# First attention stage: score groups two ahead, and a new order of the work on TensorE, VectorE and ScalarE

## The reference, cut to what matters

```python
qkv = x @ w_qkv.T                                  # 16 heads of 32
scores = q @ k.T * 32 ** -0.5 + alibi              # causal: masked scores are -10000
num = 0.5 * (1 + scores * rsqrt(1 + scores * scores))
probs = num / (sum(num) + 1e-6)                    # rational softmax
out = (probs @ v) @ w_out.T
```

## Time and profile before

| | us |
|---|---|
| median of 3 runs | 3233.4 |
| the profiled execution | 3229.13 |
| its span | 3227.3 |
| first stage, from the first values product to the first OUT product behind iteration 7 | 52.34 to 732.59 |
| cross attention and experts | the rest |

### The profile page before, as it was taken

How to read it: one execution, slowest core, us unless ns; L and a number is a source line. 1 busy time by engine, 2 the same in 40 slices (tenths; PEclk the granted TensorE clock), 3 DMA queues, 4 the chain that set the end, 5 groups by cost and what they waited for, 6 DMA issues and landing times. The chain is left out here.

```text
span 3227.3 us, 50841 instructions
## 1 busy us (share of the span) xinstructions
PE 3018.3 (94%) x19312; PEld 2477.8 (77%) x19312; DVE 1646.6 (51%) x3608; ACT 1348.0 (42%) x2298; POOL 700.2 (22%) x721
## 2 busy tenths in 40 slices
PE   5889998978999999999999949999999999999997
PEld 4667777756788777778777738888888888888886
DVE  5888888873556556666566633333333333333321
ACT  5677777764555555555555511111111111111111
POOL 0000000011111221112121033243434343434332
PEclk9889999989999999999999969999999999999999
DMA  3011111123111111111111022141313131313122
GB/s 100 24 35 44 37 45 45 46 82 121 42 50 38 45 38 56 51 38 42 41 52 34 25 74 75 54 97 55 96 55 96 56 95 56 95 57 94 57 71 37
DMA packets 93875, 189.72 MB, mean 59 GB/s; under 512 B 17568, under 2 KB 27552, under 8 KB 91712
## 3 DMA queue, kind: packets, MB, share of 16 engines
q1 hardware_dynamic: 79168, 158.68, 16.1%
q0 software_dynamic: 14592, 29.43, 5.1%
HBM read 140.25 MB, written 47.82 MB: 58 GB/s over the span
## 5 line engine op out<-in xcount | busy, mean ns | idle before, releaser
L1777 ACT ACTIVATE f_hf<-f_h 128x448 f32<-128x448 f32 x256 | 139.4, 544 | 1014.1 <-PE f_h L1804 958.0
L1748 DVE CAST f_hh<-f_hf 128x448 fp32r<-128x448 f32 x256 | 105.9, 414 | 847.0 <-ACT f_hf L1777 822.0
L1819 PE MATMUL f_y<-f_w2h,f_hh 128*128 128x512 f32 x896 | 357.5, 399 | 0.0
L1819 PE MATMUL f_y<-f_w2h,f_hl 128*128 128x512 f32 x896 | 354.0, 395 | 0.0
L1819 PE MATMUL f_y<-f_w2l,f_hh 128*128 128x512 f32 x896 | 352.2, 393 | 0.0
L1707 POOL TENSOR_TENSOR f_w1l<-f_raw,f_w1h 128x512 fp32r<-128x512 f32 x128 | 182.4, 1425 | 778.6 <-DVE f_w1h L1731 778.5
L1396 ACT ACTIVATE c_s_sb<-c_s_sb,c_nmx 112x750 f32<-112x750 f32 x256 | 236.1, 922 | 159.6 <-DVE c_nmx L1239 156.6
L1388 ACT COPY c_pT<-psum 125x672 f32<-125x672 f32 x256 | 184.6, 721 | 224.3 <-PE psum L1496 223.2
L1804 PE MATMUL f_h<-f_xTh,f_w1h 128*128 128x448 f32 x1024 | 255.2, 371 | 2.9 <-DVE f_xTl L1736 1.4
L1496 PEld LDWEIGHTS psum<-a_ident,c_s_sb 112*125 112x125 f32 x1536 | 193.5, 189 | 79.9 <-issue 76.2
L1804 PE MATMUL f_h<-f_xTl,f_w1h 128*128 128x448 f32 x1024 | 250.7, 366 | 0.0
(11 more groups left out here) (252 smaller groups left out, 5766.6 us busy)
## 6 DMA issues: line engine op xcount, KB each, us to landing
f_raw<-in_w SPq DMA_DIRECT2D x128, 512.0 KB, 4.2
h_craw<-in_ctxT SPq DMA_DIRECT2D x16, 1125.0 KB, 5.1
a_x_in<-in_x SPq DMA_DIRECT2D x9, 896.0 KB, 5.5
a_xr<-in_x SPq DMA_DIRECT2D x8, 896.0 KB, 6.0
x_dram<-a_xr SPq DMA_DIRECT2D x8, 896.0 KB, 4.8
q_dram<-a_q SPq DMA_DIRECT2D x32, 224.0 KB, 5.4
h_q<-q_dram SPq DMA_DIRECT2D x16, 448.0 KB, 5.4
c_x<-x_dram SPq DMA_DIRECT2D x16, 448.0 KB, 4.9
```

What stands on the lines that cost most here:

```text
L1748: dve.tensor_copy(hs[0][:, l % 2, c * HC:c * HC + HC], hf[:, c, :]).then_inc(h_hi, 1)
L1777: act.activation(hf[:, c, :], H[:, 0:HC], ACT.Gelu_apprx_tanh).then_inc(free, 1)
L1819: mm = pe.matmul(Y[t][:], hs[a][:, l % 2, 128 * t:128 * t + 128], w2s[b][:, l % NSLOT, :], start=j == 0 and q == 0, stop=last_of_expert(l) ...
```

## The change

`PLAN` is laid out anew, with K3 and Q3 earlier (Q3 goes to the slot 7 before, K3 to slot 0) and OUT1 in slot 4 beside OUT0. On TensorE a slot is now: values s, first half, scores of group s+2, second half. On VectorE it is: output s and its low part, transposes, `refine`, product of group s+2, first residual, `root_error` (the old L490), second residual, numerator of group s+2, then the statistics. On ScalarE: reciprocal s, off_diagonal s+1, first half's evacuations, high part of output s, `root_of`, roots of group s+2, second half's evacuations, normalise. `normalise(1, ...)` is cut in two halves, one in slot 1 and one in slot 2. The SP queue's code is unchanged. Number and size of the instructions of an iteration stay the same.

```diff
@@ -218,25 +218,25 @@
-    PLAN = {0: (["Q3", "T2c3"], ["OUT2", "OUT3"]),
-            1: (["K3"], ["V2", "V3", "T1c0"]),
+    PLAN = {0: (["K3", "T2c3"], ["OUT2", "OUT3"]),
+            1: (["V2"], ["V3", "T1c0"]),
             2: (["Z0", "T1c1"], ["Z1"]),
             3: (["Z2", "T1c2"], []),
-            4: (["Z3", "T1c3"], ["OUT0"]),
-            5: (["Q0", "T2c0"], ["K0", "OUT1"]),
-            6: (["Q1", "T2c1"], ["K1", "V0"]),
-            7: (["V1", "T2c2"], ["Q2", "K2"])}
-    PLAN_LAST = {0: (["Q3", "T2c3"], ["OUT2", "OUT3"]),
-                 1: (["K3"], ["V2", "V3"]),
+            4: (["Z3", "T1c3"], ["OUT0", "OUT1"]),
+            5: (["Q0", "T2c0"], ["K0", "Q1"]),
+            6: (["K1", "T2c1"], ["V0", "Q2"]),
+            7: (["V1", "T2c2"], ["K2", "Q3"])}
+    PLAN_LAST = {0: (["K3", "T2c3"], ["OUT2", "OUT3"]),
+                 1: (["V2"], ["V3"]),
                  2: (["Z0"], ["Z1"]),
                  3: (["Z2"], ["Z3"]),
-                 4: (["T2e0"], ["OUT0"]),
-                 5: (["T2e1"], ["OUT1"]),
+                 4: (["T2e0"], ["OUT0", "OUT1"]),
+                 5: (["T2e1"], []),
                  6: (["T2e2"], ["CK00", "CK01", "CK10"]),
                  7: (["T2e3"], ["CK11", "CK20"])}
                "second": ("T2c3", "Z0", "Z1", "Z2", "Z3")}
-    START = ["T1c0", "T1c1", "T1c2", "T1c3", "Q0", "K0", "Q1", "K1", "V0", "V1", "Q2", "K2"]
+    START = ["T1c0", "T1c1", "T1c2", "T1c3", "Q0", "K0", "Q1", "K1", "V0", "V1", "Q2", "K2", "Q3"]
     def units(kind, s, half):
@@ -485,9 +485,11 @@
             dve.wait_ge(r_made, i * NG + n + 1)
             dve.tensor_tensor(num[n % 2], sc[0:R, :, 0:NPAIR], r_sb, ALU.mult).then_inc(p_made, 1)
-        def numerator(i, n):
+        def root_error(i, n):
             dve.wait_ge(rr_made, i * NG + n + 1)
             dve.scalar_tensor_tensor(u_sb, u_sb, 1.0, q_sb, ALU.add, ALU.mult).then_inc(m_made, 1)
+
+        def numerator(i, n):
             dve.wait_ge(p_made, i * NG + n + 1)
             dve.wait_ge(m_made, i * NG + n + 1)
             dve.scalar_tensor_tensor(num[n % 2], u_sb, 3.0, num[n % 2], ALU.subtract, ALU.mult).then_inc(y_made, 1)
@@ -510,14 +512,15 @@
                               ALU.subtract).then_inc(o_lo, 1)
         def residual(i, kind, unit, n):
-
             j = int(unit[3])
             dve.wait_ge(xr_loaded, n * 16 + 16)
             dve.wait_ge(gen_full, product_number(i, kind, unit) + 1)
             b = BANK[kind, unit]
             dve.tensor_tensor(xr[:, j, :], xr[:, j, :], gen[b][0:R, :], ALU.subtract).then_inc(gen_free[b], 1)
-            dve.wait_ge(gen_free[b], uses_before(i, kind, unit) + 1)
-            statistics(1, xr, j, stats_made[1])
+
+        def residual_statistics(i, kind, unit):
+            dve.wait_ge(gen_free[BANK[kind, unit]], uses_before(i, kind, unit) + 1)
+            statistics(1, xr, int(unit[3]), stats_made[1])
         def lo_of_weights(k):
             dve.wait_ge(w_hi, k + 1)
@@ -544,33 +547,41 @@
         aggregate(0, stats_first, 2)
         product_signed(0, 0)
         refine(0, 1)
+        root_error(0, 0)
         numerator(0, 0)
+        product_signed(0, 1)
+        root_error(0, 1)
+        numerator(0, 1)
         for n in range(4, len(pieces)):
             split_piece(n)
         def body(i, kind):
             for s in range(NG):
-                late = [u for u in units(kind, s - 1, 1) if u[0] == "T"] if s > 0 else []
-                if s > 0:
-                    lo_of_output(i, s - 1)
-                elif kind != "first":
-                    lo_of_output(i - 1, NG - 1)
-                for unit in late:
-                    lo_of_transpose(i, kind, unit)
-                if has_step(kind, s + 1):
-                    product_signed(*step(i, s + 1))
-                    numerator(*step(i, s + 1))
+                for unit in units(kind, s - 1, 1) if s > 0 else ():
+                    if unit[0] == "T":
+                        lo_of_transpose(i, kind, unit)
+                output(i, s)
+                lo_of_output(i, s)
+                for unit in units(kind, s, 0):
+                    if unit[0] == "T":
+                        lo_of_transpose(i, kind, unit)
                 if s == 0 and kind in ("second", "mid"):
                     refine(0, i + 1)
                 if s == 1 and kind != "first":
                     refine(1, i - 1)
-                output(i, s)
-                for unit in units(kind, s, 0):
-                    if unit[0] == "T":
-                        lo_of_transpose(i, kind, unit)
-                for unit in units(kind, s, 1):
-                    if unit[:3] == "OUT":
-                        residual(i, kind, unit, i - 1 if unit in ("OUT2", "OUT3") else i)
+                outs = [u for u in units(kind, s, 1) if u[:3] == "OUT"]
+                if has_step(kind, s + 2):
+                    product_signed(*step(i, s + 2))
+                for unit in outs[:1]:
+                    residual(i, kind, unit, i - 1 if s == 0 else i)
+                if has_step(kind, s + 2):
+                    root_error(*step(i, s + 2))
+                for unit in outs[1:]:
+                    residual(i, kind, unit, i - 1 if s == 0 else i)
+                if has_step(kind, s + 2):
+                    numerator(*step(i, s + 2))
+                for unit in outs:
+                    residual_statistics(i, kind, unit)
                 if s == 0 and kind != "first":
                     aggregate(1, stats_made[1], i)
                 if s in (6, 7) and kind != "last":
...
@@ -596,12 +607,13 @@
             act.wait_ge(mv_made[half], n * TPI + TPI)
             act.activation(rstd[half][:], mv[half][:, :, 1], ACT.Abs_reciprocal_sqrt, bias=eps[0:R, 0:1]).then_inc(root_made[half], 1)
-        def normalise(half, n, src, dst):
+        def normalise(half, n, src, dst, *js):
             act.wait_ge(rstd_made[half], n + 1)
-            for j in range(TPI):
+            for j in js or range(TPI):
                 ins = act.activation(dst[:, j, :], src[:, j, :], ACT.Identity, bias=shift[half][:, j:j + 1],
                                      scale=rstd[half][:, j:j + 1])
-            ins.then_inc(xn_made[half], 1)
+            if j == TPI - 1:
+                ins.then_inc(xn_made[half], 1)
         def hi_of_transpose(i, kind, unit):
             dst, c = (xT if unit[1] == "1" else x2T), int(unit[3])
@@ -680,39 +692,35 @@
         for unit in ("V0", "V1"):
             evacuate(0, "start", unit)
         off_diagonal(0, 0)
-        evacuate(0, "start", "Q2")
+        roots(0, 1)
+        for unit in ("Q2", "K2"):
+            evacuate(0, "start", unit)
+        evacuate(0, "start", "Q3")
         for n, (src, dst, k) in enumerate(pieces[4:], 4):
             act.wait_ge(w_loaded[4 + n % 4], 16 * (n // 4 + 1))
             act.copy(dst[0][:, k, :], work[:, n % 4, :]).then_inc(w_hi, 1)
-        evacuate(0, "start", "K2")
         normalise(0, 1, x_in, x_in)
         def body(i, kind):
             for s in range(NG):
-                if s > 0:
-                    hi_of_output(i, s - 1)
-                elif kind != "first":
-                    hi_of_output(i - 1, NG - 1)
+                reciprocal(i, s)
                 if has_step(kind, s + 1):
-                    roots(*step(i, s + 1))
+                    off_diagonal(*step(i, s + 1))
+                for unit in units(kind, s, 0):
+                    evacuate(i, kind, unit)
+                hi_of_output(i, s)
                 if s == 0 and kind in ("second", "mid"):
                     root_of(0, i + 1)
                 if s == 1 and kind != "first":
                     root_of(1, i - 1)
-                reciprocal(i, s)
-                for unit in units(kind, s, 0):
+                if has_step(kind, s + 2):
+                    roots(*step(i, s + 2))
+                for unit in units(kind, s, 1):
                     evacuate(i, kind, unit)
-                late = units(kind, s, 1)
-                for unit in late[:1]:
-                    evacuate(i, kind, unit)
-                if s == 1 and kind in ("second", "mid"):
+                if s == 0 and kind in ("second", "mid"):
                     normalise(0, i + 1, x_in, x_in)
-                if s == 2 and kind != "first":
-                    normalise(1, i - 1, xr, xn2)
-                if has_step(kind, s + 1):
-                    off_diagonal(*step(i, s + 1))
-                for unit in late[1:]:
-                    evacuate(i, kind, unit)
+                if s in (1, 2) and kind != "first":
+                    normalise(1, i - 1, xr, xn2, 2 * s - 2, 2 * s - 1)
                 if kind == "last" and s in (2, 4):
                     for n in range(3):
                         handover.hi_of_piece(act, n + 3 * (s // 4))
...
@@ -846,31 +853,35 @@
         run(0, "start", "K1")
         made(0, "start", "Q0", "K0")
         scores(0, 0)
-        for unit in START[8:]:
+        for unit in ("V0", "V1"):
             run(0, "start", unit)
```

(31 more changed lines are left out.)

## The result

| | before | after |
|---|---|---|
| median, us (range) | 3233.32 (3229.09 to 3235.1) | 3293.59 (3290.99 to 3294.36) |
| the profiled execution | 3229.13 | 3293.21 |
| first stage, to the first OUT product behind iteration 7 | 732.59 | 799.76 |

The ratio is 1.0191, with a 95% interval of 1.0178 to 1.0204: the changed kernel is slower, by about 1.9%. The forecast was 3287, within 3250 to 3312.

The account below looks back on a forecast made before the run. A closed 9.92 us loop through ScalarE and VectorE was taken as the bound. Iterations 2 to 6 +45.3, iteration 1 +6.3, iteration 0 +2.5, iteration 7 +2: +56 on 3229.13, plus 2 for the median, gives 3287 us, range 3250 to 3312.

Parts of the forecast that it names:

- The loop is not opened; a slot costs at least 9.92: ScalarE-VectorE ring from `o_made` through high part, roots and numerator to the next output: stays closed, at least 9.92 us a slot.
- Residuals and statistics: VectorE, slots 0 and 4: two units each now stand between L486 and the next output, +2.27 us a slot.
- `aggregate`, statistics of x, T1c0, `root_of`: Work moved into the loop, us (slots): `aggregate` 0.48 (0, 7), x 1.19 (6, 7), T1c0 0.54 (1), `root_of` 0.2 (0, 1).
- T1c1 and the low clock: Slot 2: TensorE's T1c1 waits for T1c0's low part, then group 4's scores run at half clock, delaying roots: +1.26 us.
- Z2 behind the store: Slot 3, iterations 2 to 6: ScalarE's Z2 evacuation waits for Z0's store, holding up high part and roots: +4.0 us.
- Start and iteration 0: Before the first `o_made`: 0, bounds -4 to +4 us; iteration 0, `o_made` 0 to 7: 74.7 against 72.19, +2.5 us.
- Iteration 7: Last iteration, up to the first OUT product: 91.6 us against 89.65, +2 us.
- The signs: Wrong if L486 waits under 2 us in slots 3 and 5; TensorE's waits for `o_made` should grow.
- Rival A: Loop rules, but the T1c1 low-clock and Z0-store ties are not met: 28 us less, 3259; chance 0.17.
- Rival B: TensorE's trailing eats its 1.5 us in three slots of six iterations: +27 us, 3312; chance 0.12.
- Rival C: Two-group lead ends TensorE's waits, its own work bounds: iteration 77.2 us or less, -45 us, 3186; chance 0.07.
- Rival D: The change moves the waits and no time, each addition replacing an equal wait: 3233 us; chance 0.02.

Follow-up runs that it names:

- experiment 5: Changed kernel with Z0's store early, roots s+2 and first-half evacuations earlier on ScalarE, low parts of output and late transposes behind root_error on VectorE; 3186.33 us, ratio 0.9868.
- Experiment 8: Kernel before, lead of one group kept: roots s+1 ahead of high part of output s-1, low part between root_error and numerator; 3244.48 us, ratio 1.0034.
- experiments 3 and 4: Changed kernel plus two VectorE statistics in slot 5: in 3 behind the numerator, 3307.92 us; in 4 ahead of the product, 3294.78 us.
- experiment 1: Changed kernel with the store of Z0 issued on the SP queue ahead of the wait for normalise and the load of xr; 3274.05 us, ratio 1.0133.
- experiment 2: Changed kernel with T1c0's low part on VectorE moved from behind slot 1's numerator to between root_error and numerator; 3283.66 us, ratio 1.0165.
- experiment 7: Experiment 5 with the last iteration's four loads of the next stage's weights ahead of Z0's store and the wait for normalise; 3180.04 us, ratio 0.9848.

## Why the prediction held, step by step

The mechanism held; that the total came so close is partly luck. Up to the first OUT product behind iteration 7 the profiled execution grew by 67.2 us where 56 was forecast, 8.9 of the difference in iteration 7, and the later stages' -3.2 hid part of it.

- **The loop is not opened; a slot costs at least 9.92.** Right, and shown from both sides. Slot 5 is 9.92 or 9.93 in every iteration, no slot of a full iteration is under it, and experiment 5 has slots of 7.6 and 8.2. It takes away the tie on ScalarE (roots behind the high part) and leaves the one on VectorE (output behind the numerator). Experiment 8, with nothing but the roots and the low part moved, took slot 3 of the kernel before from 9.93 to 8.07, so these two moves together open the loop.
- **Residuals and statistics, +2.27.** Measured 12.11 less 9.92 = 2.19. That it is the place and not the work that costs was shown by experiments 3 and 4, on the statistics; the residuals have only the slots of the changed kernel as evidence.
- **`aggregate`, statistics of x, T1c0, `root_of`.** Slots 0, 1, 6 and 7 were forecast at 12.87, 10.66, 11.11 and 11.59 and measured at 12.76, 10.64, 11.12 and 11.92. Only slot 7 was off, by 0.33 in iterations 2 to 5; in iterations 0, 1 and 6 it was 11.58 to 11.60. The same 0.3 stays in experiment 1, so Z2's wait isn't its cause, nor is TensorE: VectorE's first instruction of the output starts 0.61 to 0.65 us behind the start of `aggregate` in these four and 0.29 in the others, in a gap that no wait fills. Those four are the passes at whose end the program's loop (it runs iterations 2 to 6) goes back to its start; that this jump is the cause fits, but was not tried.

```profile
427.76 0.38 DVE L462 BATCH_NORM_AGGREGATE a_mv<-a_stats 112x2 f32<-112x6 f32 x4
428.39 0.39 DVE L503 SCALAR_TENSOR_TENSOR a_dt<-psum,a_rden 128x224 f32<-128x224 f32 x1 [0.25 <-issue]
```

- **T1c1 and the low clock, +1.26.** TensorE idled 5.51 us where "some 5" was said, and the granted clock behind it was 0.50. Slot 2 lost 1.46, and experiment 2 gave 1.45 back. The term was 0.2 too small.
- **Z2 behind the store, +4.0.** Slot 3 measured 3.74 to 4.24 more than 9.92 in iterations 2 to 6 and nothing more in iteration 1, which has no Z. Experiment 1 gave it all back in these iterations. What stands ahead in the queue is what the store's time was made of, as the prediction argued: 6.15 us behind the load of `xr`, so the row was the one to take. The rule of the Trainium skill's page "DMA: Bandwidth & Descriptors", section "Anatomy of one DMA", about 2.0 us plus bytes over 436 GB/s for the software-driven path, gives an estimate of 2.5 us for 224 KB and would have had slot 3 only 0.6 over the loop. The store issued by itself in experiment 1 landed in 2.1 us, not far from it; behind the load it did not.
- **Start and iteration 0.** 0.85 and 2.7, forecast 0 and 2.5.
- **Iteration 7: the one term that was mis-sized.** +10.9 against +2. Slots 0 to 2 came as forecast (12.57, 10.11 and 17.55 against 12.67, 10.12 and 17.8). Slot 3 took 15.32 where 9.92 stood, slot 4 14.49 where 12.19 stood, and from `o_made` 6 to the first OUT product it was 8.95 instead of 7.4. The first of them, in ScalarE's timeline: Z2 waited for its store here too, which the forecast had only for iterations 2 to 6. It puts the high part of output 3, which could have started at the end of its output at 751.08, at 752.74.

```profile
752.30 0.54 ACT L646 ACTIVATE a_q<-psum 128x448 f32<-128x448 f32 x1 [2.69 <-DMA q_dram<-a_q]
752.74 0.37 ACT L672 CAST a_oTh<-a_o_sb 128x224 fp32r<-128x224 f32 x1
```

  That is 1.6 us, and in experiment 1 slot 3 was 13.71, 1.6 less (slot 2 was 0.8 longer there, where the weights came later). What is left of slots 3 and 4, 3.8 and 2.4 us, is VectorE's own instructions taking longer, below. Slot 2 holds 0.8 of the same (L506 takes 1.18 instead of 0.39 from 749.90 on), so that it came out at 17.55 is partly luck; the wait for the weights was 6.6 instead of 7.2. The 1.55 by which the last stretch ran over was not followed.
- **The signs.** L486 waited 1.7 us in slots 3 and 5, under the 2 that the prediction had set as a sign of being wrong. The sign was set wrongly: the low part of a transpose (0.6 us) lies under the cover in these slots and takes up part of the wait, while from the start of the high part to L486 it is still 3.06 us (384.45 to 387.51, in slot 4) against 3.05. TensorE's waits for `o_made` were to grow and fell, from 53.2 to 35.2 us; what grew instead is its wait for the low part of the transposes (T), 49.4 us:

```profile
PE psum L839 <- DVE a_o_sb L506: 35.2, 13, 9.4
PE psum L763 <- DVE a_xTl L481: 49.4, 12, 8.2
```

- **The chances.** Rival A's two ties were both met. Rival B has no row for it: ScalarE's roots waited for scores 7 times in the stage, 6.2 us in all, which is the T1c1 wait of slot 2 and nothing else. (Its 3312 adds 27 to 3285; from the 3287 of the forecast it is 3314.) Rival C at 0.07 described a kernel one step away from this one, and it was right to hold it low for these lists. That experiment 5 ended at its 3186 is partly luck: against the kernel before iterations 2 to 6 gained 29.4 where C had 35.5, iteration 1 gained 3.8 where it had 6, and iteration 0 gained 8.2 where it had 3. Rival D had its reason stated and failed by it.

## What to carry to other kernels

Cut a pipelined loop at one semaphore and ask of each slot which engines it goes round; where two in-order lists close a ring, work inside the ring costs its full time and work in the gap nothing until the gap is full (experiments 3 and 4), whatever the mean busy shares say. In this kernel more lead for a third engine brought nothing while the ring was closed, and opening the ring brought nothing while that engine had a lead of one group (experiment 8); so try both together. A moved evacuation or high part also moves behind every wait on its new way, a DMA store's among them.

## What the runs showed of the hardware

In iteration 7 of the changed kernel VectorE's instructions take up to twice their time. Its timeline, and GpSimd's beside it:

```profile
757.25 1.55 DVE L490 SCALAR_TENSOR_TENSOR a_ew<-a_ew 112x1344 f32<-112x1344 f32 x1
758.90 2.97 DVE L495 SCALAR_TENSOR_TENSOR a_ew<-a_ew 112x1344 f32<-112x1344 f32 x1
761.91 2.58 DVE L497 SCALAR_TENSOR_TENSOR a_ew<-a_ew,a_keep 112x896 f32<-112x896 f32 x1
...
771.55 2.52 DVE L490 SCALAR_TENSOR_TENSOR a_ew<-a_ew 112x1344 f32<-112x1344 f32 x1
774.00 0.67 DVE L519 TENSOR_TENSOR a_xr<-a_xr,psum 112x512 f32<-112x512 f32 x1
```
```profile
758.32 7.84 POOL L108 TENSOR_TENSOR h_cTl<-h_craw,h_cTh 128x750 fp32r<-128x750 f32 x3 [7.50 <-ACT h_cTh L103]
771.39 6.35 POOL L94 TENSOR_TENSOR h_wvl<-h_stage,h_wvh 128x512 fp32r<-128x512 f32 x3 [5.24 <-ACT h_wvh L89]
```

L495 took 1.56 elsewhere and L497 1.09, while the same GpSimd work spans 5.54 and 3.90 us in the kernel before, where it meets only short instructions of VectorE (they grow too, L504 from 0.39 to 1.65). Both engines lose while they overlap, and ahead of 758.32 L490 has its usual 1.55. Only instructions that read both inputs from SBUF are long; L519, which reads one of them from PSUM, has its usual 0.67 in the midst. The excess of L495, L497 and L506 in slot 3 adds up to 3.8 us, that of L490, L495 and L497 in slot 4 to 2.4. By the Trainium skill's page "SBUF — State Buffer", section "Who interferes with whom", a VectorE instruction with two inputs in SBUF contends with a GpSimd instruction that reads SBUF; the trace agrees. In the loop this time counts in full. No experiment here took GpSimd's work away, but experiment 7 moved it: its first group starts at 638.09, spans 5.39 us instead of the 3.73 of experiment 5, and meets `numerator`'s last instruction, which takes 2.07 us instead of the 1.09 of experiment 5.

TensorE's work for one iteration is not a constant. The same list (690 to 696 of its matmuls are in the records) was busy for 77.21 us at a granted clock of 0.96, 80.89 at 0.93 in the changed kernel and 75.38 at 1.00 in experiment 5: an order that takes waits away gave back nearly 2 us of an iteration in the matmuls themselves.
